# First attention of a two-layer decoder: zeros written into the probabilities by GpSimd in place of mask products on TensorE

## The reference, cut to what matters

```python
qkv = x @ W_qkv + b_qkv
q, k, v = jnp.split(qkv, 3, axis=-1)          # 16 heads of 16
coef = jnp.einsum('bhqd,bhkd->bhqk', q_h, k_h) / scale
causal = jnp.tril(jnp.ones((n_tokens, n_tokens), dtype=bool))
coef = jnp.where(causal[None, None], coef, -jnp.inf)
attn = jax.nn.softmax(coef, axis=-1)
att_h = jnp.einsum('bhqk,bhkd->bhqd', attn, v_h)
return att @ W_out + b_out
```

## Time and profile before

| what | value |
|---|---|
| median of 3 runs | 2494.14 us (2493.24 to 2495.34) |
| the profiled execution's own time | 2495.48 us |
| its span, first to last instruction | 2494.2 us |
| busy, PE / DVE / ACT / POOL | 89% / 86% / 75% / 43% of the span |
| mean granted TensorE clock | 0.978 |
| exponentials of the first attention | 66.7 to 524.7 us |
| the three other blocks | from about 527 us on |

### The profile page before, as it was taken

One profiled execution on the slowest core, in us unless ns is written; L12 is line 12 of the kernel. 1 busy time (PEld: TensorE's weight loads), 2 busy tenths in 40 slices (PEclk: granted clock), 3 DMA queues, 4 the chain that ended last, 5 costly groups with the idle time before them and its releaser, 6 DMA issues.

```text
span 2494.2 us, 50463 instructions
## 1 busy us (share of the span) xinstructions
PE 2217.1 (89%) x18456; PEld 1580.5 (63%) x18544; DVE 2148.6 (86%) x3182; ACT 1864.8 (75%) x2640; POOL 1073.9 (43%) x1480
## 2 busy tenths in 40 slices
PE   4888888869997899999999999999999999988899
PEld 2444444445554567777777777777767767766587
DVE  6888888858896899999999999999999999988521
ACT  4877777746666588888888888888888888878411
POOL 3312111101213475665665656656656656632200
PEclk9999999989998899999999999999999999999899
DMA  3000000040000399999999999999999999999100
GB/s 127 1 2 1 2 1 1 2 96 20 1 1 1 62 183 191 193 193 191 191 191 194 194 191 191 197 185 195 195 191 190 193 193 189 202 196 198 42 17 17
DMA packets 1119317, 300.67 MB, mean 121 GB/s; under 512 B 1107232, under 2 KB 1116416, under 8 KB 1118208
## 3 DMA queue, kind: packets, MB, share of 16 engines
q1 hardware_dynamic: 1116224, 295.21, 68.2%
q10 hardware_dynamic: 2848, 2.23, 0.3%
HBM read 18.45 MB, written 2.10 MB: 8 GB/s over the span
## 4 chain that ended last, share of the span: by engine, by line
DVE 29%; PE 21%; issue 10%; ACT 5%; DMA 2%; SPq 0%; DVEq 0%; ACTq 0%
DVE lows L1601 13%; DVE parts L1617 13%; PE psS L1552 3%; PE psOb L1472 3%; PE psS L1455 2%; DMA partsT<-parts 2%; PE psS L1456 2%; PE psS L1457 2%; ACT parts L1801 2%; PE psOb L1508 1%; PE psOb L1473 1%; ACT prob L1791 1%; PE psOb L1572 1%; PE psPb L1572 1%; DVE shift L1609 1%
## 5 line engine op out<-in xcount | busy, mean ns | idle before, releaser
L1791 ACT ACTIVATE prob<-psS,shift 128x1024 f32<-128x1024 f32 x512 | 574.3, 1122 | 171.2 <-DVE shift L1609 161.7
L1617 DVE TENSOR_TENSOR parts<-prob,parts 128x1024 f16<-128x1024 f32 x512 | 661.0, 1291 | 23.2 <-ACT parts L1801 20.1
L1601 DVE TENSOR_REDUCE lows<-psS 128x1 f32<-128x1024 f32 x512 | 621.3, 1213 | 4.9 <-PE psS L1457 4.7
L1801 ACT CAST parts<-prob 128x1024 f16<-128x1024 f32 x512 | 536.7, 1048 | 19.7 <-DMA partsT<-parts 15.8
L1455 PE MATMUL psS<-k_hi,q_lo 128*128 128x512 f32 x1024 | 449.7, 439 | 100.0 <-ACT prob L1791 92.8
L1472 PEld LDWEIGHTS psOb<-kv,partsT 128*128 128x128 f16 x4096 | 356.6, 97 | 91.4 <-issue 75.3
L1472 PE MATMUL psOb<-kv,partsT 128*128 128x130 f16 x4096 | 396.7, 221 | 12.7 <-DMA partsT<-parts 12.4
L1456 PE MATMUL psS<-k_lo,q_hi 128*128 128x512 f32 x1024 | 407.3, 398 | 0.0
L1457 PE MATMUL psS<-k_hi,q_hi 128*128 128x512 f32 x1024 | 406.8, 397 | 0.0
L1473 PE MATMUL psOb<-kv,partsT 128*128 128x66 f16 x4096 | 386.5, 192 | 0.0
L1473 PEld LDWEIGHTS psOb<-kv,partsT 128*128 128x128 f16 x4096 | 360.1, 98 | 1.0 <-issue 1.0
(11 more groups left out here) (293 smaller groups left out, 3913.5 us busy)
## 6 DMA issues: line engine op xcount, KB each, us to landing
partsT<-parts SPq DMA_TRANSPOSE x512, 4.8
ef<-in_ewT SPq DMA_DIRECT2D x1, 2048.0 KB, 10.3
rf<-in_rwT SPq DMA_DIRECT2D x1, 2048.0 KB, 10.0
outw_s<-in_outwT SPq DMA_DIRECT2D x1, 2048.0 KB, 8.7
trig<-in_trig SPq DMA_DIRECT2D x2, 1024.0 KB, 11.2
out_x<-ot SPq DMA_DIRECT2D x16, 128.0 KB, 1.7
wug<-in_wupT SPq DMA_DIRECT2D x4, 256.0 KB, 3.9
wug<-in_wgateT SPq DMA_DIRECT2D x4, 256.0 KB, 3.8
```

The lines of the kernel that those rows point to most:

```text
L1601: dve.tensor_reduce(lows[:, n % 2, g:g + 1], psS[:, (2 * n + g) % 3, :], AX_X, ALU.min).then_inc(half_min, 1)
L1617: dve.tensor_tensor(parts[:, s, 1, :], prob[:, g, :], parts[:, s, 0, :], ALU.subtract).then_inc(low_done, 1)
L1791: act.activation(prob[:, g, :], psS[:, (2 * n + g) % 3, :], ACT.Exp, bias=shift[:, n % 2:n % 2 + 1], scale=-1.0).then_inc(exp_done, 1)
L1801: act.copy(parts[:, s, 0, :], prob[:, g, :]).then_inc(high_done, 1)
```

## The change

The scores for the exponentials are no longer masked. After each of the two diagonal exponentials of a unit, GpSimd writes zeros into the parts above the diagonal of the two blocks in PT, in place, by an affine_select of 128 x 128 bf16. It waits for `exp_done` first and raises the new semaphore `cleared` after each block, on which it waits before the next. PE's wait at `pv`, r = 0, is for the unit's fourth block on `cleared`. In the products for the maxima the mask stays. The diff:

```diff
@@ -211,6 +211,7 @@
         score_ready, exp_done = sem("a_score_ready"), sem("a_exp_done")
+        cleared = sem("a_cleared")
@@ -362,18 +363,15 @@
                     for m, off, r in pieces:
                         w = BANK - r * P
                         bank = psS[:, x * BANK + off - first:x * BANK + off - first + w]
-                        diag = m >= 4 * c
                         ins = pe.matmul(bank, kT[:, pair % 2, m * P:(m + 1) * P],
-                                        qB[:, h, c * BANK + r * P:(c + 1) * BANK], start=True, stop=not diag)
-                        if diag:
-                            ins = pe.matmul(bank[:, 0:P], maskb[:, :], identb[:, :], start=False, stop=True)
+                                        qB[:, h, c * BANK + r * P:(c + 1) * BANK], start=True, stop=True)
                     ins.then_inc(score_ready, 1)
...
                     if r == 0:
-                        pe.wait_ge(exp_done, done["exp", pair, c, h, 2 * c + 1])
+                        pe.wait_ge(cleared, 4 * unit(pair, c, h) + 4)
@@ -606,6 +604,15 @@
                     pool.wait_ge(rested_b, part + 1)
+                elif kind == "exp":
+                    pair, c, h, q = at
+                    if q >= 2 * c:
+                        pool.wait_ge(exp_done, n["exp"] + 1)
+                        for m, off, _ in exp_pieces(c, q):
+                            block = PT[:, h, off:off + P]
+                            pool.affine_select(out=block, in_=block, pattern=[[1, P]], compare_op=ALU.is_ge, fill=0.0,
+                                               base=0, channel_multiplier=-1).then_inc(cleared, 1)
+                            pool.wait_ge(cleared, 4 * unit(pair, c, h) + m - 4 * c + 1)
```

## The result

The changed kernel took 2503.2 us (median of 6 runs, 2500.65 to 2505.89), the kernel before 2495.22 us (6 runs). The ratio is 1.0034, 95% interval 1.0023 to 1.0044: slower by 8 us, where +8.9 us and 2503.0 us were forecast. How far the terms behind that sum were right is another matter: the last pair was put too high, the drops of the clock in the later pairs had no term, and the two errors partly cancelled.

What follows compares the result with a forecast made beforehand. No engine paces alone: PE-DVE and PE-ACT loops share PE's in-order queue, so whatever stops PE stops all three. -3.4 + 7.5 + 0.5 + 4.3 = +8.9 us on 2494.14 gives 2503.0 us; range 2494 to 2525.

Steps and rivals of the forecast that it cites:

- Masks, -3.4 us: First attention's scores: 256 mask products go, 13.7 us of PE stream, of which one round in four counts: -3.4 us.
- Price of a block, 0.50 us with its wait: POOL: one 128x128 clear takes 0.43 us like a two-input product, plus 0.07 wait; 2.0 us a unit.
- No cost in the pairs between: Steady state: clears need 2.3 us, covers before PE's weighted products are 2.5 to 4.0 us, so 0, narrowly.
- The threshold of 0.55 us a block: Steady state: from this block price the cover is gone and PE's wait for the clears shows in every unit.
- the covers: Time from a unit's 896-wide exponential to PE's first weighted load, 2.5 to 4.0 us, in which clears cost nothing.
- the slow rival: POOL too slow: at 1.06 + 0.07 us a block every unit waits; +103 us, 2597 us; chance 0.20.
- Pair 0, +7.5 and +0.5 us: Unit (0,1,0): clears queue behind POOL's 8.84 us subtraction, PE stands 8.4 us, net +7.5; lower granted clock after it +0.5.
- The 0.9 us taken back: Pair 0: deducted from PE's 8.4 us stop because PE before stopped again for ACT, 81.01 to 81.92.
- The last pair, +4.3 us: No maxima left to cover the clears: the last three units delay PE by 1.5, 1.0 and 1.8 us, +4.3 us.

Runs made afterwards that it cites:

- e1: The changed kernel without its clears, so that nothing masks the probabilities; 2491.16 us, ratio 0.9985 to the kernel before.
- e4: The changed kernel with the big cast and subtraction moved from pair 0's unit (0,1,0) to (0,3,0); 2495.67 us, ratio 0.9998 to the kernel before.
- e7: e4 with PE waiting for the clears one by one instead of all four at r = 0; 2492.24 us, ratio 0.9994 to the kernel before.
- e6: The changed kernel with every clear made twice, 0.73 us a block; 2514.57 us, ratio 1.0087 to the kernel before.
- e3: The kernel before, masks kept, no clears; PE waits at unit (0,1,0) for the end of GpSimd's big subtraction; 2506.48 us, ratio 1.0040.
- e2: The changed kernel with the mask products put back, so clears are added alone; 2506.34 us, ratio 1.0041 to the kernel before.
- e8: e7 with one affine_select clearing both blocks of a diagonal exponential, PE waiting by twos; 2494.12 us, ratio 0.9999 to the kernel before.

## Why the prediction was right

By its own steps:

**Masks, -3.4 us: right.** e1 shows -4.0 us by the medians, 0.43 us of 1.71 in a pair at the full clock. Reading which of DVE's gaps follow an unbroken run of PE through masked scores gave the share of one in four; PE's busy share or the 27 us that ACT waits for line 369 would not have.

**Price of a block, 0.50 us with its wait: mis-sized**, 0.36 measured (0.294 and 0.07). The instruction belongs beside the one-input copy (0.29), not beside the two-input product; that it compares an index costs nothing that shows. The estimate of 0.30 to 0.40 us from the Trainium skill (GPSIMD Engine Reference, Performance pitfalls) held at its lower end; the estimate of 1.5 us by its branching figure is five times what was measured.

**No cost in the pairs between: right**, and with more room than thought: e4's and e7's 56.47 us equal e1's. The threshold of 0.55 us a block was too sharp, though. At 0.73 us (e6) a pair loses 0.3 us where the covers gave 1.1; that DVE and ACT have the rest in hand while PE stands is argued. So the slow rival was priced too dear near its threshold; its price at 1.13 us a block was not tested.

**Pair 0, +7.5 and +0.5 us: right in place and mechanism**, with two errors of opposite sign inside. By the same steps with the true block price the load is 7.8 us late, and it was: it went 1.56 us behind the unit's last exponential before and 9.26 after, 7.7 us later. The 0.9 us taken back was wrong: e3 paid 6.1 of its 6.26 us. Between the same two exponentials as in e3 the changed kernel takes 14.4 us (78.05 to 92.42) against 6.3, so the stop cost 8.1 us. The clock is left with some 0.4 of it, where 0.5 was set: PE works 5.1 us at the 1.2 GHz level after the stop (85.0 to 90.1), against 3.4 us in the kernel before. e3 shows the wait alone, e4 its removal.

**The last pair, +4.3 us: mis-sized**, for two reasons. With the true block price the terms of the three units are 0.9, 0.4 and 1.3 us, 2.6 in all. Measured at the full clock are 0.6, 0.1 and 1.1, together 1.8 us; e7 against e4 gives the same. PE's loads went later by 0.8, 0.85 and 1.1 us, less than the 1 to 2 us expected, and of the first two together less than half reached the exponentials.

**What had no term: the clock in the later pairs.** In the changed kernel's profile four of the pairs 1 to 6 hold a stretch at the lower level, in that of before three, and a pair at full clock gains 0.4 us, so the six pairs gave back only 1.6 us where six times 0.43 were there to be had. One more lies at the end of pair 0 and costs 0.4 us there. In e2 and e3, with the masks, the same costs 1.1 us a pair. Added up, 8.1 for the stop, 1.8 for the last pair, -3.4 for the masks (eight pairs at 0.43) and 1.4 for these drops are 7.9 us, where 8.0, 4.3, -3.4 and nothing were forecast. The drops made up for part of the last pair's smaller loss. That the sum is within a microsecond of the forecast is therefore partly luck.

What stays open: why the stretch at the lower clock comes back in all of e3's pairs and not in all of before's, and how often each does so. PE has a lull at the end of every pair, in e3 1.86 us of waiting for DVE before 128.76, and the clock falls behind it; but the kernel before has the same lull without a fall (290.10 to 293.50, PE 1.68 us busy, the clock 1.00). Over many executions only the mean clock of each is known, 0.975 to 0.982 in before.

## What to carry to other kernels

Before work is given to an idle engine, read what else stands in that engine's queue, once for the whole kernel and not for the steady state: here 256 new instructions were free in the pairs between, and one old subtraction of 8.8 us ahead of four of them made the change a loss. A long background job on an engine that gets a place in a tight loop should be cut into pieces or moved first, with a control of the move alone. And let the consumer wait for the part that it needs next, not for the whole.

## What the runs showed that was not expected

A drop of the granted clock can fall in step with a loop: in e3 it recurred every 58.0 us from 128.8 us on, one in each pair, and cost 1.1 us each (58.0 against 56.9 us; 57.3 against 56.5 without the masks). It is tempting to say that e3's stall set them off, and it is not shown. Kernels without the stall have such rows too: e1 has three drops 58.0 us apart,

```profile
290.80:294.20 3.40, 3.40 (x12) 1.26 (x11) 2.94 (x6) 1.41 (x2) 0.00 (x0) 0.50 0.00 0
348.80:352.20 3.40, 3.26 (x10) 1.27 (x11) 2.49 (x6) 1.63 (x3) 0.00 (x0) 0.50 0.00 0
406.80:410.20 3.40, 3.36 (x11) 1.29 (x12) 2.53 (x5) 1.67 (x3) 0.00 (x0) 0.50 0.00 0
```

and e8 has four. And in e2, which has the stall, the last one is at 362.1 and the pair from 422.58 on has none. What e3 shows is that they can last through a whole stage: its wait cost 6.1 us and its median rose by more than 10.
